# Selective scan on one core: decays from differences of running sums in two-part fp32r products

## The chip, the cores and the metric

The program runs on one core of a Trainium2 chip. Its engines work side by side, each through its own queue in order: TensorE (PE, matrix products into PSUM), VectorE (DVE), ScalarE (ACT, activation functions from tables), GpSimd (POOL) and SyncE (SP, which here only starts transfers). The metric is the device time of one execution in microseconds (us), as the median of several runs; lower is better. PE's weight loads are shown apart from its products, as PEld. An fp32 product shows as two passes with a weight load each, an fp32r product as one.

## The reference

Two layers over 4 x 2048 tokens of width 256: attention with LoRA and a small mixture of experts, then a chunked selective state-space scan and a second mixture of experts. Only the scan is touched by the change. Its core, cut to what matters (one head group, 4 heads of width 128, state width 64, `dA = dt * A`, all negative):

```
cum = jnp.cumsum(dA, axis=2)
seg = cum[:, :, :, None, :] - cum[:, :, None, :, :]
decay = jnp.where(tri[None, None, :, :, None], jnp.exp(seg), 0.0)
scores = jnp.einsum('bcin,bcjn->bcij', Cc, Bc)
att = scores[..., None] * decay * dtc[:, :, None, :, :]
y_intra = jnp.einsum('bcijh,bcjhp->bcihp', att, xc)
```

The kernel scans in sub-tiles of 128 tokens, so for each sub-tile and head it needs a 128 x 128 table `exp(cum_i - cum_j)`, masked to the triangle.

## The kernel before

The program is a row of stages; `scan_phase` is the fifth, and runs from about 3590 to 4468 us of the span. It goes through 16 chunks of 512 tokens (4 batches of 4 chunks, the batch being the hardware loop, the chunks written out in it). I call the work of one pass a turn. In turn `i` the kernel scans chunk `i`, in 4 sub-tiles s = 0 to 3; it projects, convolves and gates chunk `i + 1`; and it normalizes chunk `i + 2`. Each engine's order within a turn is written out by hand.

PE writes most results into four PSUM banks `sc_ps_a`, used in rotation. The list `A_TURN` says in which order: its names are `xT` (inputs transposed), `dt` (step sizes), `seg` (decay exponents), `ct` (convolution inputs), `z` (gates), `gT` (gated rows transposed), `out` (output projection), `cum` (sums), `uT` (normalized inputs transposed). PE may write entry k once ACT has read entry k - 4 (`into`, semaphore `a_out`), and ACT reads entry k once PE has written it (`take`, `a_done`). So PE and ACT follow the same list and are never more than four entries apart.

The decays of a sub-tile are made like this. POOL computes the step sizes by a series of short operations (`softplus_argument`, `softplus_series`), and its last operation gives `dA` (L1520). ACT multiplies a strictly lower triangular mask by `dA`, head by head (`segment_mask`, L1773, four activations a sub-tile). PE multiplies each of the four masks by an upper triangular one in fp32 (`decays`, L1966), which gives the exponents. ACT takes their exponential (L1784, `sc_decay`), DVE multiplies by the scores (L1658, `sc_att`), and PE uses the result in `own` (L2002).

The names that matter below: `own` 0 is PE's product for sub-tile 0 of the turn; DVE adds it up (L1675), whereupon POOL gates the row (`gate`, L1534). POOL's order in a turn is gate 0, `second_root` (L1488), in the first turn of a batch the weights `wob` (L1527), the step sizes, `dA`, gates 1, 2 and 3. PE needs gate s for `gT`s (L2018). In PE's order `gT1` comes just before `sums` (L1958) and, before the change, `seg0` of the next chunk. Near the turn's end PE does z3 (L1943), gT2, uT0, the scores of the next chunk (L1976), uT1 (L1927), the state of sub-tile 3 (L2011), gT3, out2, out3 (L2027) and xT0 (L1984). The product for out3 waits until ACT has copied gT3 (L1829). The step-size products (L1950, four columns each) and `seg1` come right after the next turn's start.

ACT's exponential and its Silu lie in different function tables; a change from one to the other shows as ACT_TABLE_LOAD. Copy, Identity and Square need no change.

## Time and profile before

| what | value |
|---|---|
| median of 3 runs | 5099.54 us (5083.22 to 5102.6) |
| the profiled execution | 5088.73 us |
| its span, first to last instruction | 5087.2 us |
| mean granted clock of TensorE | 0.942 of 2.4 GHz |
| scan stage, about | 3590 to 4468 us of the span |
| PE busy over the whole span | 92% |
| DVE, ACT, POOL busy over the whole span | 84%, 69%, 27% |

Times within the trace are counted from the span's start. A busy share says how much of a stretch an engine worked; a wait says who came last. In the scan a turn takes 48.5 to 55.8 us, by ACT's copies of the step sizes at 3711.6, 3761.8, 3812.1, 3860.8 and 3916.5 us and so on.

### The profile page before, as it was taken

What the parts mean: (1) busy time and instruction counts of PE and PEld (TensorE: products, weight loads), DVE (VectorE), ACT (ScalarE), POOL (GpSimd) and SP (SyncE); (2) the same over time, 40 slices, a digit from 0 to 9 for tenths busy, and PEclk for the clock granted to TensorE, in tenths of its full rate; (3) what the DMA queues carried; (4) which work ended last, traced back from release to release, by engine and by line L of the source; (5) the groups of instructions that cost most, each with busy time, mean ns of one, the idle gap of its engine ahead of it and who ended that gap; (6) DMA issues with size and microseconds to landing.
All of it is one profiled execution on the core that took longest, in us unless ns stands there. A gap on an engine that the chain in (4) does not pass through costs nothing. (4 is left out here: it accounts for less than half of the span.)

```text
span 5087.2 us, 109400 instructions
## 1 busy us (share of the span) xinstructions
PE 4686.5 (92%) x35413; PEld 2578.5 (51%) x35413; DVE 4257.3 (84%) x6858; ACT 3489.3 (69%) x6724; POOL 1383.5 (27%) x1285
## 2 busy tenths in 40 slices
PE   5869999999999999999999879999699999956998
PEld 4723333333333333333333367777466666655887
DVE  5769999999999999999999868887677877875554
ACT  2438888888888888888888722322477777844554
POOL 1121111111111111111111133333334344445776
PEclk8959999999999999999999989999799999956999
DMA  4962222122222222222222111111000000044452
GB/s 157 345 146 43 52 44 49 39 47 52 44 47 42 46 52 43 44 44 45 55 44 44 33 51 41 37 50 37 22 25 24 28 20 23 25 162 148 164 164 94
DMA packets 236446, 340.01 MB, mean 67 GB/s; under 512 B 60199, under 2 KB 169762, under 8 KB 227340
## 3 DMA queue, kind: packets, MB, share of 16 engines
q1 hardware_dynamic: 219760, 275.26, 22.3%
q0 software_dynamic: 16192, 58.43, 3.1%
q8 instruction: 277, 4.54, 0.4%
q14 instruction: 217, 1.78, 0.1%
HBM read 205.49 MB, written 136.18 MB: 67 GB/s over the span
## 5 line engine op out<-in xcount | busy, mean ns | idle before, releaser
L816 DVE TENSOR_REDUCE at_mxp<-at_ps_m 128x2 f32<-128x1024 f32 x2092 | 2524.5, 1221 | 72.9 <-PE at_ps_m L869 53.0
L747 ACT ACTIVATE at_prob<-at_ps_s 128x512 f32<-128x512 f32 x4100 | 2228.2, 596 | 326.8 <-PE at_ps_s L859 261.7
L879 PE MATMUL at_ps_o<-at_prob,at_vs 128*32 128x256 f32 x16384 | 1313.9, 392 | 14.1 <-ACT at_osum L753 14.1
L859 PE MATMUL at_ps_s<-at_qs,at_ks 51*128 51x512 f32 x4100 | 1036.5, 500 | 5.2 <-ACT at_prob L747 5.2
L869 PE MATMUL at_ps_m<-at_ks,at_qs 49*128 49x512 f32 x4184 | 856.3, 405 | 46.5 <-DMA at_ks<-t_alibi 35.7
L859 PEld LDWEIGHTS at_ps_s<-at_qs,at_ks 51*128 51x128 f32 x4100 | 384.9, 183 | 856.6 <-ACT at_prob L747 856.1
L879 PEld LDWEIGHTS at_ps_o<-at_prob,at_vs 128*32 128x32 f32 x16384 | 323.1, 108 | 775.3 <-issue 388.5
L574 POOL TENSOR_TENSOR at_total<-at_total,at_minus 128x16 f32<-128x16 f32 x65 | 190.4, 2929 | 1118.1 <-DMA at_total<-at_osum 1118.1
L869 PEld LDWEIGHTS at_ps_m<-at_ks,at_qs 49*128 49x128 f32 x4184 | 404.0, 190 | 67.9 <-DMA at_ks<-t_alibi 36.1
L68 DVE TENSOR_TENSOR ex_hidc<-ex_hid,ex_hidc 128x512 fp32r<-128x512 f32 x128 | 158.0, 1245 | 168.9 <-ACT ex_hid L2561 168.9
L1321 PE MATMUL mi_ps_f<-mi_w,mi_act 128*128 128x256 f32 x1024 | 252.6, 391 | 15.7 <-DVE mi_acc L1179 15.7
L1244 ACT ACTIVATE mi_act<-mi_ps_h,mi_b 128x512 f32<-128x512 f32 x130 | 89.5, 688 | 233.2 <-PE mi_ps_h L1310 232.8
L1179 DVE SCALAR_TENSOR_TENSOR mi_acc<-mi_ps_f,mi_mask,mi_acc 128x256 f32<-128x256 f32 x512 | 215.1, 475 | 36.6 <-PE mi_ps_f L1321 32.9
L1310 PE MATMUL mi_ps_h<-mi_hTc,mi_w1c 128*128 128x512 f32 x780 | 236.5, 441 | 7.6 <-POOL mi_hTc L68 7.6
L569 POOL TENSOR_TENSOR at_nparts<-at_nmax,at_nparts 128x16 fp32r<-128x16 f32 x65 | 14.4, 222 | 798.5 <-DVE at_nparts L823 798.5
L2560 ACT ACTIVATE ex_hidc<-ex_ps_h,ex_b 128x512 fp32r<-128x512 f32 x128 | 88.2, 689 | 202.9 <-PE ex_ps_h L2591 202.9
L1321 PEld LDWEIGHTS mi_ps_f<-mi_w,mi_act 128*128 128x128 f32 x1024 | 196.5, 196 | 58.9 <-DVE mi_acc L1179 29.4
L1634 DVE SCALAR_TENSOR_TENSOR sc_cv<-sc_xc,sc_conv_w,sc_cv 128x512 f32<-128x512 f32 x255 | 198.6, 812 | 19.0 <-issue 5.9
L578 POOL TENSOR_TENSOR at_onorm<-at_osum,at_weight 128x512 f32<-128x512 f32 x65 | 83.4, 1283 | 338.0 <-DMA at_weight<-t_inverse 338.0
L1310 PEld LDWEIGHTS mi_ps_h<-mi_hTc,mi_w1c 128*128 128x128 f32 x780 | 152.1, 199 | 44.8 <-issue 14.0
L1937 PE MATMUL sc_ps_a<-sc_uT,sc_win 128*128 128x512 f32 x340 | 166.7, 624 | 0.9 <-ACT sc_uT L1821 0.9
L1534 POOL TENSOR_TENSOR sc_g<-sc_ysum,sc_sz 128x512 f32<-128x512 f32 x64 | 83.0, 1297 | 293.1 <-DVE sc_ysum L1675 293.1
(317 smaller groups left out, 6443.5 us busy)
## 6 DMA issues: line engine op xcount, KB each, us to landing
t_parts<-pr_parts SPq DMA_DIRECT2D x64, 512.0 KB, 7.1
at_ks<-t_parts SPq DMA_DIRECT2D x102, 256.0 KB
t_buf<-at_blank POOLq DMA_DIRECT2D x64, 384.5 KB, 3.2
at_qs<-t_parts SPq DMA_DIRECT2D x96, 256.0 KB
at_vs<-t_v SPq DMA_DIRECT2D x17, 1024.0 KB, 5.0
ex_rest<-t_buf SPq DMA_DIRECT2D x16, 1026.0 KB, 5.3
t_v<-pr_vaug SPq DMA_DIRECT2D x64, 256.0 KB, 5.5
first_w<-in_fw SPq DMA_DIRECT2D x16, 1024.0 KB, 7.6
```

Source lines behind the costliest of these rows:

```text
L68: return eng.tensor_tensor(out, src, upper.bitcast(F32), ALU.subtract)
L574: nc.gpsimd.tensor_tensor(total[:, :], total[:, :], minus[:, :], ALU.pow).then_inc(inverted, 1)
L747: nc.scalar.activation(prob[0 if up is None else (t + 1) % 2][:, j, :], ps_s[bank][:, :], ACT.Exp).then_inc(s_read, 1)
L816: nc.vector.tensor_reduce(out[:, s4, k + i, 2 * pair:2 * pair + 2], ps_m[i][:, :, :], AX.X, ALU.max).then_inc(mx_read, 1)
L859: nc.tensor.matmul(ps_s[bank][:, :], ks[s][a:a + QROWS, j // 2, t1 * P:(t1 + 1) * P], qs[s][a:a + QROWS, j // 2, c * T:(c + 1) * T], start ...
L869: last = nc.tensor.matmul(ps_m[i][:, a, :], qs[s][a * 64:a * 64 + MXR, pair, q0:q0 + P], ks[s][a * 64:a * 64 + MXR, pair, (k + i) * T:(k + ...
L879: last = nc.tensor.matmul(ps_o[32 * j:32 * j + 32, q0:q1], vs[s][:, t, 32 * j:32 * j + 32], prob[t % 2][:, j, q0:q1], start=(t == 0 and ha ...
L1179: last = nc.vector.scalar_tensor_tensor(acc[:, s, :], ps_f[pair][:, j, :], mask[h][:, s, e:e + 1], acc[:, s, :], ALU.mult, ALU.add)
L1310: last = nc.tensor.matmul(ps_h[e % 2][:, :], w1c[a][:, e, k, :], hTc[h][r][:, k, :], start=(k == 0 and n == 0), stop=(k == KD - 1 and n == 2))
L1321: last = nc.tensor.matmul(ps_f[pair][:, j, :], act_e[e][:, s * P:(s + 1) * P], w2[:, e, :], start=True, stop=True)
L1634: last = nc.vector.scalar_tensor_tensor(cv[:, ct, :], xc[h][:, ct, k:k + T], conv_w[:, ct, k:k + 1], cv[:, ct, :], ALU.mult, ALU.add)
L1937: last = nc.tensor.matmul(bank[:, :], win[:, k, DI + ct * P:DI + (ct + 1) * P], uT[h][:, k, :], start=(k == 0), stop=(k == KD - 1))
```

## The change

The decay exponents come from differences of running sums. With `run` the running sum of `dA` over the tokens (rows: 4 sub-tiles x 4 heads), an exponent is `run[i] - run[j]`. To keep precision in fp32r, `run` is split in two parts, a rounded one and the rest, as 48 rows (part, sub-tile, head; the middle part is zero).

- POOL writes `dA` twice (into parts 0 and 2 of `dA_rows`).
- PE's `sums` gets a fourth fp32 product, 48 x 128, which gives the running sums as rows.
- ACT's `sums` copies these rows twice (once rounded to fp32r), and after its exponential drains and scales the rounded ones by -1 in part 2 only.
- POOL's new `running_rows`, between gate 2 and gate 3, adds the two into `run` (48 x 128) and spreads them over heads into `spread_run` (48 x 512).
- PE's `decays` is two accumulating fp32r products with 512 columns and 48 rows, in place of four fp32 products with 128 columns.
- ACT's `segment_mask`, four times four activations a turn, is gone.
- Without the mask, exponents above the diagonal are positive; DVE caps the decay at 1 in the instruction that applies the scores, whose triangle is masked as before.
- `seg0` of the next chunk moves behind z3 in PE's order, in ACT's order and in the rotation of banks.
- Ahead of the loop SP loads four small tables, and POOL converts two of them.

```diff
-          + ["gT1", "cum", "seg0", "z2", "out1", "z3", "gT2", "uT0", "uT1", "gT3", "out2", "out3", "xT0"])
+          + ["gT1", "cum", "z2", "out1", "z3", "seg0", "gT2", "uT0", "uT1", "gT3", "out2", "out3", "xT0"])
...
+                sp.dma_start(decay[0][0:CR, :, :], x["own_rows"].rearrange("r (s c) -> r s c", s=SUB)).then_inc(rows_in, 16)
...
-                    nc.gpsimd.tensor_tensor(dA[h][:, :, :], dts[h][:, :, :], a_neg[:, :].unsqueeze(1).to_broadcast([P, SUB, NH]), ALU.mult).then_inc(dA_done, 1)
+                    for part in (0, 2):
+                        last = nc.gpsimd.tensor_tensor(dA_rows[h][:, part, :, :], dts[h][:, :, :], a_neg[:, :].unsqueeze(1).to_broadcast([P, SUB, NH]), ALU.mult)
+                    last.then_inc(dA_done, 1)
+
+                def running_rows(n, h):
+                    pool.wait_ge(run_out, n + 1)
+                    nc.gpsimd.tensor_tensor(run[h][:, :], run_m[:, :], run_f[:, :], ALU.add)
+                    pool.drain()
+                    nc.gpsimd.tensor_tensor(spread_run[h][:, :, :], run[h][:, :].bitcast(F32).unsqueeze(1).to_broadcast([CR, NH, P]),
+                                            head_rows[:, :].unsqueeze(2).to_broadcast([CR, NH, P]), ALU.mult).then_inc(run_set, 1)
...
                         gate(i, h, 2, True)
+                        running_rows(i + 1, 1 - h)
                         gate(i, h, 3, True)
...
-                    nc.vector.tensor_tensor(att[r][:, :, :], decay[r][:, :, :], sm[r][:, :].unsqueeze(1).to_broadcast([P, NH, P]), ALU.mult).then_inc(att_done, 1)
+                    nc.vector.scalar_tensor_tensor(att[r][:, :, :], decay[r][:, :, :], 1.0, sm[r][:, :].unsqueeze(1).to_broadcast([P, NH, P]), ALU.min, ALU.mult).then_inc(att_done, 1)
...
-                def segment_mask(n, h, s, used):
...
                 def sums(turn, h):
                     bank = take(turn, "cum")
+                    nc.scalar.copy(run_r[:, :], bank[0:CR, P:2 * P])
+                    nc.scalar.copy(run_f[:, :], bank[0:CR, P:2 * P])
                     nc.scalar.activation(ex[h][:, :, :, :], bank[:, 0:3 * SUB * NH].rearrange("p (a s h) -> p a s h", a=3, s=SUB), ACT.Exp).then_inc(a_out, 1)
+                    act.drain()
+                    nc.scalar.activation(run_m[:, :], run_r[:, :].bitcast(F32), ACT.Copy, scale=minus_low[:, 0:1]).then_inc(run_out, 1)
...
                         gate_squares(i, h, 1)
-                        decays(turn, i + 1, 0, True)
-                        segment_mask(i + 1, 1 - h, 1, place(turn, "seg3")[0])
                         gates(turn, 1 - h, 2)
...
                         gates(turn, 1 - h, 3)
+                        decays(turn, i + 1, 0, True)
                         gated_columns(turn, 2)
...
-                    pe.wait_ge(seg_set, i * SUB + s + 1)
-                    for k in range(NH):
-                        last = nc.tensor.matmul(bank[:, k * P:(k + 1) * P], segm[s % 2][:, k, :], upper[:, :], start=True, stop=True)
-                    last.then_inc(a_done, 1)
+                    pe.wait_ge(run_set, i + 1)
+                    nc.tensor.matmul(bank[:, :], own_rows[:, s, :], spread_run[h][:, :, :].rearrange("r h c -> r (h c)"), start=True, stop=False)
+                    nc.tensor.matmul(heads(bank), run[h][:, :], minus_rows[:, s, :].unsqueeze(2).to_broadcast([CR, NH, P]), start=False, stop=True).then_inc(a_done, 1)
```

On ACT, from the gate z3 (L1808) to the copy of gT3 (L1829), the order before was this. `sc_sz` is a Silu, `sc_xs` the Silu of the convolution.

```order
L1808 ACTIVATE sc_sz<-sc_ps_a 128x512
L1829 COPY sc_gT<-sc_ps_a 128x512
L1821 ACTIVATE sc_uT<-sc_ps_a,sc_nb,sc_nw 128x512
L1813 ACTIVATE sc_xs<-sc_cv 128x512
L1821 ACTIVATE sc_uT<-sc_ps_a,sc_nb,sc_nw 128x512
L1829 COPY sc_gT<-sc_ps_a 128x512
```

The same stretch, from z3 to the copy of gT3, in the changed kernel:

```order
L1831 ACTIVATE sc_sz<-sc_ps_a 128x512
L1807 ACT_TABLE_LOAD
L1807 ACTIVATE sc_decay<-sc_ps_a 128x512
L1852 COPY sc_gT<-sc_ps_a 128x512
L1844 ACTIVATE sc_uT<-sc_ps_a,sc_nb,sc_nw 128x512
L1836 ACT_TABLE_LOAD
L1836 ACTIVATE sc_xs<-sc_cv 128x512
L1844 ACTIVATE sc_uT<-sc_ps_a,sc_nb,sc_nw 128x512
L1852 COPY sc_gT<-sc_ps_a 128x512
```

The exponential of `seg0` now stands between two Silus, with a table load on each side of it. Before, it shared a table with the exponentials of `seg3` and `sums`.

On PE, from gT1 to z2, the order before was:

```order
L2018 MATMUL sc_ps_a<-ident,sc_g 128x128 x4
...
L1958 MATMUL sc_ps_a<-sc_dA,upper 128x16
L1958 MATMUL sc_ps_a<-sc_dA,sc_lower 128x16
L1958 MATMUL sc_ps_a<-sc_dA,ones 128x16
...
L1966 MATMUL sc_ps_a<-upper,sc_segm 128x128 x4
...
L1943 MATMUL sc_ps_a<-sc_win,sc_uT 128x512 x2
```

and in the changed kernel:

```order
L2033 MATMUL sc_ps_a<-ident,sc_g 128x128 x4
...
L1974 MATMUL sc_ps_a<-sc_dA,upper 128x16
L1974 MATMUL sc_ps_a<-sc_dA,sc_lower 128x16
L1974 MATMUL sc_ps_a<-sc_dA,ones 128x16
L1975 MATMUL sc_ps_a<-upper,sc_dA 48x128
...
L1959 MATMUL sc_ps_a<-sc_win,sc_uT 128x512 x2
```

A fourth product of `sums` has come in, and `seg0` has left this place for the one behind z3.

## Rows read from the trace of the kernel before

**Rows 1.** Stretches of the scan: busy time by engine, clock, DMA share, GB/s.

```profile
3700.00:3800.00 100.00, 99.50 (x490) 66.83 (x491) 79.01 (x206) 78.10 (x192) 42.03 (x60) 0.97 0.08 25
```

**Rows 2.** Waits of PE, then of ACT, from 3700 to 4400 us.

```profile
PE sc_ps_a L2018 <- POOL sc_g L1534: 8.9, 8, 2.4
...
ACT sc_segm L1773 <- POOL sc_dA L1520: 25.5, 14, 3.6
```

**Rows 3.** Timeline of PE, one turn: start, us, engine, line, tiles, count [wait].

```profile
3767.63 1.05 PE L2002 MATMUL sc_ps_y<-sc_xdt,sc_att 128*128 128x128 f32 x8
...
3788.77 1.09 PE L2011 MATMUL sc_ps_st<-sc_xdt,sc_btw 128*64 128x128 f32 x8
3790.11 0.63 PE L2018 MATMUL sc_ps_a<-ident,sc_g 128*128 128x128 f32 x4 [0.25 <-POOL sc_g L1534]
...
3791.17 1.14 PE L1966 MATMUL sc_ps_a<-upper,sc_segm 128*128 128x128 f32 x8
3792.14 1.88 PE L1943 MATMUL sc_ps_a<-sc_win,sc_uT 128*128 128x512 f32 x4
...
3797.73 1.88 PE L1943 MATMUL sc_ps_a<-sc_win,sc_uT 128*128 128x512 f32 x4
...
3802.98 3.62 PE L2027 MATMUL sc_ps_a<-sc_wob,sc_gT 128*128 128x256 f32 x16
3806.44 0.60 PE L1984 MATMUL sc_ps_a<-ident,sc_xs 128*128 128x128 f32 x4
...
3816.32 1.05 PE L2002 MATMUL sc_ps_y<-sc_xdt,sc_att 128*128 128x128 f32 x8
```

**Rows 4.** Timeline of POOL in the same turn, gate 0 to gate 2.

```profile
3769.49 1.27 POOL L1534 TENSOR_TENSOR sc_g<-sc_ysum,sc_sz 128x512 f32<-128x512 f32 x1 [10.79 <-DVE sc_ysum L1675]
...
3772.66 0.22 POOL L1497 TENSOR_TENSOR sc_zp<-sc_ez,sc_two 128x16 f32<-128x16 f32 x1
...
3788.52 0.22 POOL L1520 TENSOR_TENSOR sc_dA<-sc_dts,sc_a_neg 128x16 f32<-128x16 f32 x1
3788.69 1.27 POOL L1534 TENSOR_TENSOR sc_g<-sc_ysum,sc_sz 128x512 f32<-128x512 f32 x1
3792.65 1.37 POOL L1534 TENSOR_TENSOR sc_g<-sc_ysum,sc_sz 128x512 f32<-128x512 f32 x1 [2.69 <-DVE sc_ysum L1675]
```

**Rows 5.** Timeline of PE in the expert stage: six fp32r products with 512 columns.

```profile
4699.92 1.54 PE L2591 MATMUL ex_ps_h<-ex_bTc,ex_w1c 128*128 128x512 f32 x6
4701.30 1.60 PE L2603 MATMUL ex_ps_y<-ex_w2c,ex_hidc 128*128 128x256 f32 x12
```

**Rows 6.** Timeline of ACT in the same turn, z2's table load and z3 to gT3.

```profile
3794.12 1.28 ACT L1808 ACT_TABLE_LOAD   x1
3795.41 0.60 ACT L1808 ACTIVATE sc_sz<-sc_ps_a 128x512 f32<-128x512 f32 x1
...
3799.65 0.60 ACT L1808 ACTIVATE sc_sz<-sc_ps_a 128x512 f32<-128x512 f32 x1 [1.20 <-PE sc_ps_a L1943]
3800.14 0.58 ACT L1829 COPY sc_gT<-sc_ps_a 128x512 f32<-128x512 f32 x1
3800.61 0.80 ACT L1821 ACTIVATE sc_uT<-sc_ps_a,sc_nb,sc_nw 128x512 f32<-128x512 f32 x1
3801.28 0.63 ACT L1813 ACTIVATE sc_xs<-sc_cv 128x512 f32<-128x512 f32 x1
3801.80 0.79 ACT L1821 ACTIVATE sc_uT<-sc_ps_a,sc_nb,sc_nw 128x512 f32<-128x512 f32 x1
3803.18 0.59 ACT L1829 COPY sc_gT<-sc_ps_a 128x512 f32<-128x512 f32 x1 [0.59 <-PE sc_ps_a L2018]
```

**Rows 7.** First turn of a batch: PE's timeline at gT1, then stretches with their clock.

```profile
3891.24 1.05 PE L2018 MATMUL sc_ps_a<-ident,sc_g 128*128 128x128 f32 x4 [2.40 <-POOL sc_g L1534]
...
3895.07 3.40 PE L1943 MATMUL sc_ps_a<-sc_win,sc_uT 128*128 128x512 f32 x4
...
3891.00:3898.00 7.00, 6.76 (x22) 5.21 (x23) 3.57 (x6) 4.44 (x12) 1.46 (x2) 0.52 0.00 1
3761.60:3765.00 3.40, 3.40 (x10) 2.14 (x10) 3.23 (x12) 3.37 (x9) 0.00 (x0) 0.50 0.50 146
```

More of the change, by code:

```diff
@@ L1906, in batch @@
                         projected(turn, h, 3)
-                        segment_mask(i + 1, 1 - h, 2, place(turn, "seg0")[0])
                         skip_inputs(turn, i + 1, 1 - h, 0, True)
@@ L2078, in _ @@
                         sums(turn, n, g1)
-                        decays(turn, n, 0)
                         gates(turn, g1, 2)
@@ L2084, in _ @@
                         gates(turn, g1, 3)
+                        decays(turn, n, g1, 0)
                         gated_columns(turn, 2)
```

54 lines of the change are left out of this document (33 added, 21 removed).

## The prediction

> **What bounds the kernel now.** I read the stretches of the scan first. In a typical hundred microseconds PE is busy for 99.5, DVE 79.0, ACT 78.1 and POOL 42.0 [rows 1]. That looks like a stage bound by PE alone, in which each microsecond taken from PE is a microsecond won. So I went to the waits. PE waits for one thing, POOL's gated row before gT1: 8.9 us in total, 8 times, at most 2.4 [rows 2]. That is little, but it says that at one place POOL arrives as late as PE does. The reader is to see this in the two timelines of one turn.
>
> In PE's timeline `own` 0 starts at 3767.63. The state of sub-tile 2 starts at 3788.77 and takes some 1.1, and gT1 starts at 3790.11 with a wait of 0.25 ahead of it [rows 3]. In POOL's timeline gate 0 starts at 3769.49, the step sizes at 3772.66, `dA` at 3788.52 and gate 1 at 3788.69, which takes 1.27 and ends at 3789.96 [rows 4]. PE's gT1 starts 0.15 later. From `own` 0 to gT1, stretch A, there are thus two paths of nearly the same length. One is PE's own work, 22.2 us. The other goes `own` 0, DVE, gate 0, the step sizes, `dA`, gate 1, gT1, and takes 22.5 us; almost nothing of it is PE's. The rest of the turn, stretch B, from gT1 at 3790.11 to the next `own` 0 at 3816.32, is 26.2 us [rows 3], and in it PE runs without waits. In the first turn of a batch POOL also makes `wob`, and PE's wait is 2.40 [rows 7].
>
> **The change, part by part.** *PE, the decays.* Eight fp32 passes of one sub-tile occupy PE from 3791.17 to 3792.14, 0.97 us [rows 3]. The new form is two fp32r products with 512 columns. The nearest row has six of them from 4699.92 to 4701.30, so 0.23 each and 0.46 for two [rows 5]. It contracts over 128 rows and not 48, and it repeats no column; I take it as it stands. Each sub-tile gives back 0.51. The bounds are 0.40 for the pair, if few rows were cheaper, and 1.7 if it ran at the rate of the fp32 form (four passes with 512 columns take from 3792.14 some 1.7 [rows 3]). The fourth product of `sums` is two more fp32 passes with 128 columns: 2 x 0.97 / 8 = 0.24.
>
> *Stretch A* holds the decays of sub-tiles 2 and 3, so PE's path falls from 22.2 to 21.2. POOL's path does not fall. It gets a second `dA` operation: the first starts at 3788.52 and the next operation at 3788.69, so one costs 0.17 [rows 4]; I take 0.2. It ends stretch A at 22.7. So A becomes 0.2 longer, and PE's wait at gT1 grows from 0.25 to about 1.5. The 1.0 us given back by PE is lost there.
>
> *Stretch B, PE's side.* It holds the decays 0 and 1 and `sums`: -0.51 - 0.51 + 0.24 = -0.8.
>
> *Stretch B, ACT's side.* Here the two table loads matter. A load takes 1.28 and begins only when the activation ahead has ended: from 3794.12 to the Silu at 3795.41 [rows 6]. I lay out the new order with the spacings of the rows. Since `seg0` has left and the fourth sum has come, z3 ends 0.97 - 0.24 = 0.73 earlier, and ACT's Silu of z3 starts at 3799.65 - 0.72 = 3798.93. It takes 0.60, the load 1.29, the exponential 0.49 to the next start (the spacing from z3 to gT2), gT2 0.47, uT0 0.80 (its full length, since a load follows), the load 1.29, the Silu 0.52, uT1 about 0.67 and gT3's copy 0.59 [rows 6]. The sum is 6.72, so gT3 is copied at 3805.65. PE's out3 needs it. PE would come to out3 at half of the way from 3802.98 to 3806.44, which is 3804.71, less 0.73 and plus 0.46 for `seg0` in its new place: 3804.44 [rows 3]. So PE waits for ACT by 1.2 us, where before it did not wait: ACT had gT3 copied at 3803.77 [rows 6] and out3 came 0.9 later. Out3 starts 0.94 later than before. The decays of sub-tile 1 then give back 0.51, and stretch B becomes 0.4 longer in place of 0.8 shorter.
>
> The Trainium skill, in "ScalarE: Activation LUTs", "What ACT_TABLE_LOAD costs", puts a switch at some 1283 ns of load and some 1380 ns of drain. The load agrees with the row's 1.28. Of the drain the row shows nothing beyond the end of the activation ahead, and the row decides. By the page two switches would cost 2.8 us more than I have put down, in each turn.
>
> *What is hidden.* The masks that go, sixteen activations a turn, free ACT, but ACT waited for `dA` at one of them anyway (25.5 us in 14 turns [rows 2]), and no wait of PE for a mask stands among PE's waits. ACT already stood idle for 1.20 before z3's Silu [rows 6]; that, and the two masks that went from the stretch ahead of it, covers the three new small activations in `sums`. `running_rows` costs POOL about as much as a gate, 1.27 [rows 4], and a fraction for the addition. Gate 2 ends at 3794.02 [rows 4], some 4 us after gT1, and `seg0` is asked for after z3, 8.6 us after gT1: it has 3 us to spare, and gate 3 is asked for later. DVE's cap stands in an instruction of the same size; DVE is busy for 79.0 of 100 [rows 1]. If the cover were gone, each tenth of a microsecond on DVE would count four times a turn, 6 us in all. The first chunk has the new chain sums, ACT, POOL, PE in the open in place of two masks: +1 us.
>
> **Sum.** A turn becomes 0.2 + 0.4 = 0.6 us longer, 16 turns 10, with the first chunk 11 us.
>
> *The clock.* In the stretch after the wait of 2.40 the granted clock was 0.52, the half level of 1.2 GHz, for about 7 us, and four passes took 3.40 in place of 1.88 [rows 7]. In another stretch after the small step-size products it was 0.50 for 3.4 us [rows 7]. A wait of 1.5 followed by the small products of `sums` is a case between. I cannot tell from rows whether it brings the clock down: nothing if it never does, and about 1.6 a turn if it does once in each (3.4 us at half speed), 26 us. I take two turns in five, 10 us.
>
> So +21 us. The profiled execution took 5088.7 and the median is 5099.5, with 5083.2 as the lowest; the four values centre at 5094, and I add to that: **5115 us**.
>
> **The rivals.**
>
> 1. *PE alone is the bound, and all it gives back is won.* For it: PE is busy for 99.5 of 100. Against it: the 0.25 us wait, which leaves no room in stretch A. It would need POOL's path to shorten. Four times 0.51 less 0.24 is 1.8 a turn, -29 us in all: 5065.
> 2. *ACT comes in time at gT3.* If a table load could run while PE's z3 is awaited, one of the two would be hidden, B would be shorter by 0.8 and A longer by 0.2: -10 us, 5084. Against it: the load stands behind the Silu of z3, and needs its end.
> 3. *The new waits bring the clock down in nearly every turn.* PE now waits 1.5 at gT1 and 1.2 before out3. With 1.6 to 3.2 us a turn lost at half speed, on top of 11: +37 to +62, 5131 to 5156. It decides from about one turn in two on. For it: the row after 2.40 us. Against it: most waits now are shorter than that one.
> 4. *The decays don't get cheaper.* A pair at 1.7 us adds 0.7 per sub-tile to a turn's B in place of giving 0.51 back: about 2.4 a turn, over 40 us slower. Against it: fp32r at 0.23 in the expert stage [rows 5].
>
> **How the numbers follow.** The forecast (10 us from the two waits, 0 to 26 from the clock, so 5105 to 5131) has 0.60. A third of that, 0.18, lies above +0.5%. Rival 1 has 0.09, rival 2 0.08, rival 3 0.20 and rival 4 0.03. Half a per cent is 25 us, about what a measurement of this kernel can tell from no change. Faster by more: rival 1, 0.09. Slower by more: 0.18 + 0.20 + 0.03 = 0.41. Within: 0.42 + 0.08 = 0.50. The range leaves out rival 1 and the upper end of rivals 3 and 4: 5080 to 5150.
>
> **What would show it.** In the changed profile I expect: gT1 starting 22.7 after `own` 0, with a wait for POOL of about 1.5 in each turn; six table loads a turn where there were four; out3 starting right after ACT's copy of gT3, and some 1.7 us behind its place; decays of about 0.46 on PE; PE's busy share in the scan down to about 95 of 100; and a turn of 49 to 51 us without the batch's first. I am wrong if gT1 keeps its place relative to PE's own work, if POOL's path is shorter than 22 us, or if the copy of gT3 comes before PE is through out2. I am also wrong in size if the half clock appears after gT1 in all turns or in none.

## The result, and the profile after

The changed kernel takes 5141.54 us (median of 5 runs, 5136.32 to 5158.21), against 5099.54 us before (median of 5 runs). That is 42 us longer by the medians. The ratio is 1.0102, with a 95% interval of 1.0081 to 1.0123; it is estimated from all runs and isn't the quotient of the two medians, which is 1.0082. The forecast was 5115 with a range of 5080 to 5150, some 21 us more than the 5094 that it was added to. So the sign was right and the size was half of what came, and a part of the loss lies in a stage that the forecast had no term for.

First the span and the mean granted clock of the profiled execution after.

```profile
core 0: 5140.0 us, clock 0.938
```

Then the busy row of a hundred microseconds of its scan: PE, PEld, DVE, ACT and POOL busy, PE's clock, the DMA share and GB/s.

```profile
3740.00:3840.00 100.00, 96.71 (x434) 60.51 (x434) 80.17 (x199) 73.72 (x165) 43.04 (x64) 0.97 0.08 25
```

PE was busy for 99.50 [rows 1] and is now busy for 96.71: it has less work and waits more. The waits of PE in the scan, 3700 to 4400 us (total, times, longest), say for whom:

```profile
PE sc_ps_a L2033 <- POOL sc_g L1554: 24.5, 14, 5.8
PE sc_ps_a L2042 <- ACT sc_gT L1852: 11.0, 13, 0.9
```

The first row is the wait at gT1, 8.9 us before [rows 2]. The second, ahead of out3, is new. Here is one turn in PE's timeline: `own` 0, the pair of sub-tile 2, gT1, `sums`, z2, `seg0`, gT2, the last two projections, the step sizes with the pair of sub-tile 1, and the next `own` 0.

```profile
3784.68 1.05 PE L2017 MATMUL sc_ps_y<-sc_xdt,sc_att 128*128 128x128 f32 x8
3785.66 0.49 PE L1981 MATMUL sc_ps_a<-sc_spread_run,sc_own_rows 48*128 48x512 f32 x1
3786.00 0.38 PE L1982 MATMUL sc_ps_a<-sc_minus_rows,sc_run 48*128 48x512 f32 x1
3786.30 1.98 PE L1953 MATMUL sc_ps_a<-sc_uT,sc_win 128*128 128x512 f32 x4
...
3807.26 0.63 PE L2033 MATMUL sc_ps_a<-ident,sc_g 128*128 128x128 f32 x4 [0.86 <-POOL sc_g L1554]
3807.73 0.29 PE L1974 MATMUL sc_ps_a<-sc_dA,upper 128*128 128x16 f32 x2
...
3808.75 1.98 PE L1959 MATMUL sc_ps_a<-sc_win,sc_uT 128*128 128x512 f32 x4
...
3816.25 0.49 PE L1981 MATMUL sc_ps_a<-sc_spread_run,sc_own_rows 48*128 48x512 f32 x1
3816.58 0.37 PE L1982 MATMUL sc_ps_a<-sc_minus_rows,sc_run 48*128 48x512 f32 x1
3816.89 0.66 PE L2033 MATMUL sc_ps_a<-ident,sc_g 128*128 128x128 f32 x4
...
3820.48 1.89 PE L2042 MATMUL sc_ps_a<-sc_wob,sc_gT 128*128 128x256 f32 x8
3823.16 1.99 PE L2042 MATMUL sc_ps_a<-sc_wob,sc_gT 128*128 128x256 f32 x8 [0.78 <-ACT sc_gT L1852]
3824.99 0.60 PE L1999 MATMUL sc_ps_a<-ident,sc_xs 128*128 128x128 f32 x4
...
3827.07 1.85 PE L1966 MATMUL sc_ps_a<-sc_win,sc_uT 128*128 128x4 f32 x16
3828.84 0.49 PE L1981 MATMUL sc_ps_a<-sc_spread_run,sc_own_rows 48*128 48x512 f32 x1
...
3829.76 1.45 PE L2026 MATMUL sc_ps_st<-sc_xdt,sc_btw 128*64 128x128 f32 x8
3831.14 4.98 PE L1953 MATMUL sc_ps_a<-sc_uT,sc_win 128*128 128x512 f32 x8
3835.96 1.05 PE L2017 MATMUL sc_ps_y<-sc_xdt,sc_att 128*128 128x128 f32 x8
```

Stretch A, from 3784.68 to 3807.26, is 22.58; the forecast was 22.7. The pair of sub-tile 2 takes PE from 3785.66 to 3786.30, 0.64 and not 0.46. From gT1's follower `sums` (3807.73) to z2 (3808.75) are 1.02. Stretch B, from 3807.26 to 3835.96, is 28.70. It holds a slow piece: eight passes with 512 columns take 4.98 from 3831.14, where the four at 3786.30 take 1.98. In the window around the turn's start PE is busy throughout, and its granted clock (the third number from the end) is 0.66 on average, so for a part of it at the lower of its two levels, 1.2 GHz and not 2.4:

```profile
3828.80:3833.80 5.00, 5.00 (x17) 2.97 (x18) 3.85 (x16) 3.02 (x8) 0.00 (x0) 0.66 0.50 164
```

And ACT in the same turn, from z3 to the copy of gT3:

```profile
3816.36 0.60 ACT L1831 ACTIVATE sc_sz<-sc_ps_a 128x512 f32<-128x512 f32 x1 [1.53 <-PE sc_ps_a L1959]
3816.97 1.28 ACT L1807 ACT_TABLE_LOAD   x1
3818.26 0.60 ACT L1807 ACTIVATE sc_decay<-sc_ps_a 128x512 f32<-128x512 f32 x1
3818.76 0.58 ACT L1852 COPY sc_gT<-sc_ps_a 128x512 f32<-128x512 f32 x1
3819.22 0.80 ACT L1844 ACTIVATE sc_uT<-sc_ps_a,sc_nb,sc_nw 128x512 f32<-128x512 f32 x1
3820.04 1.28 ACT L1836 ACT_TABLE_LOAD   x1
3821.33 0.63 ACT L1836 ACTIVATE sc_xs<-sc_cv 128x512 f32<-128x512 f32 x1
3821.87 0.76 ACT L1844 ACTIVATE sc_uT<-sc_ps_a,sc_nb,sc_nw 128x512 f32<-128x512 f32 x1
3822.53 0.57 ACT L1852 COPY sc_gT<-sc_ps_a 128x512 f32<-128x512 f32 x1
```

This is the chain of [rows 6] with two table loads in it. It ends at 3823.10, and out3 starts 0.06 later.

I add up the two profiled executions, whose spans are 52.8 apart. Up to the scan's first product they differ by 9.8; the diff touches nothing of what PE does there, and over all profiles of this study its length goes from 3601 to 3621, in no order that follows the edits. Without it the two are 43.0 apart. The scan, from PE's first to its last product, takes 894.8 in place of 861.5: +33.4. In it the time up to the first `own` 0 is 5.5 longer, fifteen stretches A are 3.8 longer (351.1 against 347.3), fifteen stretches B are 22.9 longer (441.3 against 418.4), and the rest is 1.2. The route stage, which the change doesn't touch either, takes 163.7 in place of 152.2: +11.5. What lies behind it gives 1.9 back.

### The profile page after: what moved, and what is told of

It reads as the page before. It is cut to its first block and busy times, and to the rows that moved or that the text cites. A ratio compares the mean times of both kernels' runs of the same rounds, so it can differ in the third digit from the quotient of the medians.

```text
span 5140.0 us, 108585 instructions
## 1 busy us (share of the span) xinstructions
PE 4696.3 (91%) x35057; PEld 2546.1 (50%) x35057; DVE 4270.2 (83%) x6858; ACT 3466.2 (67%) x6539; POOL 1412.5 (27%) x1340
## 5 line engine op out<-in xcount | busy, mean ns | idle before, releaser
L1953 PE MATMUL sc_ps_a<-sc_uT,sc_win 128*128 128x512 f32 x340 | 183.6, 677 | 0.9 <-ACT sc_uT L1844 0.9
```

The source lines that it names most:

```text
L1953: last = nc.tensor.matmul(bank[:, :], win[:, k, DI + ct * P:DI + (ct + 1) * P], uT[h][:, k, :], start=(k == 0), stop=(k == KD - 1))
```

## The experiments

The table has what I read from each. A and B are sums over fifteen turns. "Quiet B" is the shortest B of a turn, without a stretch at the half clock; for the changed kernel and for e11, where every turn has one, it is 28.69 less the 1.64 that such a stretch costs in the kernel before (27.84 against 26.20) and in e3 (28.73 against 27.08). "Half" is the time in the fifteen turns at which the clock's records stand at the half level, and "falls" in how many of the fifteen turns the clock fell behind the step-size products or beside them, at the turn's start (some expectations count the sixteenth, unfinished turn as well: 14 and 4 for 13 and 3). Times are in us. They were taken in five groups, in each of which the kernel before ran as well: it took 5099.5 beside after, 5091.1 beside e1 to e4, 5084.5 beside e5 to e8, 5092.7 beside e11 to e14 and 5092.2 beside e15 to e17. So between groups the ratios are to be compared and not the times.

| kernel | time | ratio to before, 95% | A | B | quiet B | half | falls | route |
|---|---|---|---|---|---|---|---|
| before | 5099.5 | 1 | 347.3 | 418.4 | 26.20 | 51.2 | 9 | 152.2 |
| after | 5141.5 | 1.0102 (1.0081 to 1.0123) | 351.1 | 441.3 | 27.05 | 75.1 | 13 | 163.7 |
| e1_no_loads | 5126.7 | 1.0061 (1.0038 to 1.0083) | 350.5 | 418.0 | 26.00 | 61.4 | 8 | 163.7 |
| e2_move_alone | 5136.4 | 1.0083 (1.0063 to 1.0104) | 347.0 | 459.8 | 27.17 | 92.2 | 11 | 153.6 |
| e3_short_series | 5076.2 | 0.9972 (0.9957 to 0.9986) | 327.7 | 423.6 | 27.08 | 34.1 | 10 | 151.6 |
| e4_few_steps | 5089.6 | 0.9997 (0.9985 to 1.0008) | 350.5 | 397.9 | 25.72 | 27.3 | 0 | 163.8 |
| e5_before_few_steps | 5070.8 | 0.9952 (0.9930 to 0.9975) | 349.7 | 381.8 | 24.86 | 20.5 | 0 | 153.3 |
| e6_split_steps | 5124.8 | 1.0076 (1.0054 to 1.0098) | 350.3 | 425.1 | 26.94 | 44.4 | 3 | 163.9 |
| e7_seg0_beside_seg1 | 5127.5 | 1.0064 (1.0040 to 1.0088) | 350.6 | 440.4 | 25.95 | 119.5 | 14 | 163.2 |
| e8_all | 5081.8 | 0.9985 (0.9964 to 1.0005) | 325.0 | 430.9 | 26.37 | 81.9 | 13 | 164.4 |
| e11_after_filler | 5130.6 | 1.0065 (1.0041 to 1.0090) | 350.6 | 441.6 | 27.05 | 75.1 | 13 | 151.8 |
| e12_before_filler | 5086.0 | 0.9983 (0.9969 to 0.9997) | 347.8 | 411.4 | 26.20 | 37.5 | 5 | 151.7 |
| e13_after_pool | 5084.7 | 0.9986 (0.9965 to 1.0008) | 324.8 | 434.3 | 27.31 | 44.4 | 7 | 151.8 |
| e14_before_pool | 5079.0 | 0.9980 (0.9967 to 0.9993) | 332.3 | 416.2 | 26.35 | 34.1 | 6 | 153.6 |
| e15_seg0_last | 5096.9 | 1.0001 (0.9982 to 1.0019) | 325.1 | 448.8 | 26.45 | 102.4 | 13 | 151.8 |
| e16_seg0_last_split | 5077.5 | 0.9963 (0.9944 to 0.9982) | 325.0 | 425.3 | 26.30 | 54.6 | 8 | 151.7 |
| e17_after_pool_unsplit | 5087.4 | 0.9995 (0.9974 to 1.0015) | 324.8 | 434.2 | 27.47 | 41.0 | 11 | 151.7 |

The theory is the prediction's: A is bound by POOL, B by ACT's loads, and the rest is the clock. The rivals are its rivals.

### The loads, and the move

**e1_no_loads.** In the loop, `seg0`'s exponential becomes a copy.

```diff
-                    nc.scalar.activation(decay[s % 2][:, :, :], heads(bank), ACT.Exp).then_inc(a_out, 1)
+                    nc.scalar.activation(decay[s % 2][:, :, :], heads(bank), ACT.Copy if s == 0 and turn is not None else ACT.Exp).then_inc(a_out, 1)
```

> The changed kernel, but in the loop ACT copies the exponents of seg0 in place of taking their exponential (the decays of sub-tile 0 are left out of the result), so the two table loads around it go: four a turn again. If the late copy of gT3 costs PE the time before out3, that wait goes and stretch B falls by about 1.2 us a turn at equal clock, 18 us in all: about 5122. If ACT's loads are beside the point and the loss is the clock's or the new products', stretch B stays and so does the time, about 5141. The wait for POOL at gT1 stays at 0.9 either way.

The quiet B fell from 27.05 to 26.00, and PE's only wait left in the scan was POOL's:

```profile
PE sc_ps_a L2033 <- POOL sc_g L1554: 23.9, 14, 5.8
```

So the two loads cost 1.05 a turn, some 16 us in all. The sum of B fell by more, 23.3, since the clock fell in 8 turns and no longer in 13; the ratios are 0.41% apart, some 21 us. Rival 2, ACT in time, falls. The quiet B of 26.00 says one thing more: without the loads, the cheaper decays make B only 0.2 shorter than before (26.20), where the prediction had 0.8.

**e2_move_alone.** The kernel before, with only `seg0` moved behind z3 on PE and ACT.

```diff
-          + ["gT1", "cum", "seg0", "z2", "out1", "z3", "gT2", "uT0", "uT1", "gT3", "out2", "out3", "xT0"])
+          + ["gT1", "cum", "z2", "out1", "z3", "seg0", "gT2", "uT0", "uT1", "gT3", "out2", "out3", "xT0"])
```

> The kernel before, with nothing but seg0 moved behind z3 on PE, on ACT and in the banks; masks and fp32 products stay. If the loads are the cause, they come with the move: PE waits about 0.7 us before out3, 11 us in all, and a half-clock stretch more here and there: 5110 to 5120. If the two-part form is the cause, this kernel is as fast as the one before: 5100.

The waits of PE, 3700 to 4440 us, beside the old one for POOL at gT1:

```profile
PE sc_ps_a L2027 <- ACT sc_gT L1829: 12.9, 14, 1.0
PE sc_ps_in L1991 <- issue: 6.2, 3, 2.5
```

And ACT's load for `seg0` in one turn, with what it waited for:

```profile
4296.92 1.28 ACT L1784 ACT_TABLE_LOAD   x1 [0.36 <-PE sc_ps_a L1966]
```

The quiet B rose from 26.20 to 27.17. The move alone, without any cheaper decay, makes the whole of B's quiet loss. Its ratio is four fifths of the changed kernel's (1.0083 of 1.0102), though its route stage is the short one; but that holds more than the quiet loss, since B's sum, 459.8, is the largest of all, with 92.2 us at the half clock, and the time came out above its forecast of 5110 to 5120. The `issue` row is one that the changed kernel doesn't have: PE stood for some 2 us where its loop goes back, three times, and the turns there were 57 long. The load row says more: the load started only when the product was through whose result its activation reads. Between 3700 and 4400 us ACT waited so ahead of a load nine times, 3.2 us in all.

### POOL's path

**e3_short_series.** The changed kernel with three terms fewer in the step-size series.

```diff
-                    nc.gpsimd.tensor_scalar(zp[:, :, :], zw[:, :, :], 1.0 / 17, None, ALU.mult)
-                    for k in range(15, 1, -2):
+                    nc.gpsimd.tensor_scalar(zp[:, :, :], zw[:, :, :], 1.0 / 11, None, ALU.mult)
+                    for k in range(9, 1, -2):
```

> The changed kernel with three of the eight steps of POOL's series left out (the step sizes lose their last terms): POOL's path is some 3.5 us shorter. If POOL ends stretch A, it falls from 22.5 to 21.6 in the plain turns, where PE's own work ends it, and by some 3.5 in the first turn of a batch, where the half-clock stretch after gT1 should go too: 34 us in all, about 5107. If POOL is not what PE waits for, nothing moves: 5141.

A fell to 21.66 in all but the first turns of a batch, and to 22.2 to 22.4 there. Then PE's wait for POOL was all but gone, and out3's stayed:

```profile
PE sc_ps_a L2042 <- ACT sc_gT L1852: 12.0, 14, 0.9
PE sc_ps_a L2033 <- POOL sc_g L1554: 2.1, 3, 0.7
```

So POOL does bound A. It costs 0.8 to 1.1 in a plain turn and some 3 in a batch's first, where the half clock behind gT1 went with it. The time fell below the forecast of 5107, to 5076.2, since more than A moved: B's sum fell by 17.7, with the clock falling in 10 turns, and the route stage was the short one, 151.6 in place of 163.7.

### The step-size products and the clock

**e4_few_steps** and **e5_before_few_steps.** The sixteen passes of four columns become four passes of sixteen, in the changed kernel and in the one before.

```diff
-                    for s in range(SUB):
-                        for k in range(KD):
-                            last = nc.tensor.matmul(bank[:, s * NH:(s + 1) * NH], uT[h][:, k, s * P:(s + 1) * P], win[:, k, RT * P:ZX], start=(k == 0), stop=(k == KD - 1))
+                    for k in range(KD):
+                        last = nc.tensor.matmul(bank[:, 0:SUB * NH], uT[h][:, k, 0:P], win[:, k, ZX - SUB * NH:ZX], start=(k == 0), stop=(k == KD - 1))
```

> The changed kernel with the step-size products cut from sixteen small passes to four (other step sizes come out). PE has 1.3 us less to do in stretch B: 21 us in all, about 5120, if the clock falls as before. If the half-clock stretch after them is brought on by these small passes, it goes as well, 1.6 us in fourteen turns: 44 us in all, about 5097.

> The kernel before with the step-size products cut from sixteen small passes to four, as was done to the changed kernel, which then took 5089.6 (other step sizes come out). If a part of the loss is that the clock falls after these passes in more turns of the changed kernel (14 of 15 against 9 of 15 in the profiles), this kernel gains less from the edit: 1.3 us in each turn and 1.6 in nine, 36 us in all, about 5055, and the distance between the two kernels shrinks from about 45 to about 30. If the clock has no part in the loss, the distance stays at 45: about 5045.

In neither kernel did any turn show the half clock behind the step sizes. The quiet B fell by 1.3, which is the time of the passes, and the sums of B by 43 and 37. So e4 shows the second of its two forecasts (5097; it took 5089.6). What stays between the two is B's 0.9 a turn, and the route stage. The distance of the ratios is 0.45%, some 23 us, in place of 1.02%; 11 us of it are the route stage. That the distance shrinks is as forecast. The time of e5 was not: the scan is 35 us shorter, as the forecast of 5055 asks, but in the profile the part ahead of the scan is 18 us longer than in the kernel before, and the median came at 5070.8.

**e6_split_steps.** The products of the changed kernel in two halves, with the carried product and xT1 between them.

```diff
+                        steps(turn, g1, (0, 1))
                         carried(i, h, 0)
                         token_inputs(turn, i, h, 1)
-                        steps(turn, g1)
+                        steps(turn, g1, (2, 3))
```

> The changed kernel with the step-size products in two halves, one ahead of the product with the carried state and one in the old place. PE's work is the same. If the clock falls because all sixteen small passes come together, it falls there less often: 1.6 us in up to thirteen turns, 20 us in all, about 5120. If what lowers the clock is something else near the turn's start, nothing moves: 5141.

The clock fell at this place in 3 turns of 15, where it had fallen in 13; B's sum went from 441.3 to 425.1. Of these 16 us the ratios show 0.26%, some 13 us (their intervals overlap), and the time of 5124.8 is near the forecast of 5120. The clock is worth that much here, and the order of a few short products moved it. The three falls that stay are twice as long as most before, 6.8 us at the half level, and cost 3.3 each. The runs below show that the same split need not win anything (e13 beside e17).

### Other places for seg0

**e7_seg0_beside_seg1.** `seg0` goes just ahead of `seg1`, into the next turn, so that one load serves both.

```diff
-A_TURN = (["xT1", "dt", "seg1", "ct4",
-          + ["gT1", "cum", "z2", "out1", "z3", "seg0", "gT2",
+A_TURN = (["xT1", "dt", "seg0", "seg1", "ct4",
+          + ["gT1", "cum", "z2", "out1", "z3", "gT2",
```

> The changed kernel with seg0 moved on, to just ahead of seg1 in the next turn, on PE, ACT, DVE and in the banks; everything is computed. Its exponential then shares a table with that of seg1: four loads a turn. If the loads cost 1.1 us a turn in stretch B, as with the copied exponents, this kernel has B at 26.0 without a half-clock stretch and takes about 5125. If taking the exponential itself matters, or the later decays of sub-tile 0 hold up own 0, B stays at 27.1 or grows: 5141 or more.

The quiet B fell to 25.95 and out3 did not wait. But only one turn was free of the half clock at its start; in most B was 28.9. What the loads gave came back as clock: B's sum is 440.4 in place of 441.3. The median of 5127.5 is near the 5125 that the theory asked for, but it didn't come by the theory's way. In the profile the scan is 9 us shorter than the changed kernel's, and 6 of these lie ahead of the first `own` 0.

**e8_all.** The same, with the split, and two edits to POOL's order: `wob` is made ahead of gate 0, and gate 1 is done inside the series.

```diff
+                        if c == 0:
+                            weigh_rows(b, i)
                         gate(i, h, 0, old)
                         second_root(i + 2)
-                        if c == 0:
-                            weigh_rows(b, i)
                         softplus_argument(i + 1)
-                        softplus_series(i + 1, 1 - h)
-                        gate(i, h, 1, old)
+                        softplus_series(i + 1, 1 - h, lambda: gate(i, h, 1, old))
```

> Four edits on the changed kernel: seg0 beside seg1, the step-size products in two halves, the weights wob made before gate 0 instead of after it, and gate 1 put into the series of the step sizes. If the account by stretches holds, A is PE's own 21.7, also in the first turn of a batch, B is 26.0 and few turns have a half-clock stretch: 47.7 a turn against 51.2, and 55 in the first turns: 75 us less in all, about 5065, faster than the kernel before. If the stretches were bound by something else, the gain is under 40 us.

A was 21.66 in every turn, the batch's first too. So another order of the same work on POOL is enough to free A; less work, as in e3, is not needed. The half clock stayed at the turn's start, in 13 of 15 turns and most often for 6.8 us. So the forecast of 5065 was missed by 17 us.

### The route stage

Here are POOL's rows in the route stage's second chunk, before and then after. Up to this place the two run alike.

```profile
4511.15 1.04 POOL L2171 TENSOR_TENSOR ro_rstd<-ro_ve,ro_mhalf 128x4 f32<-128x4 f32 x1 [2.36 <-DVE ro_ve L2217]
4512.19 0.19 POOL L2176 TENSOR_TENSOR ro_target<-ro_slot,ro_away 128x4 uint32<-128x4 uint32 x1
4513.60 1.21 POOL L2179 DMA_INDIRECT t_buf<-ro_row,ro_target  x1 [1.22 <-issue]
```

```profile
4554.15 1.04 POOL L2186 TENSOR_TENSOR ro_rstd<-ro_ve,ro_mhalf 128x4 f32<-128x4 f32 x1 [2.36 <-DVE ro_ve L2232]
4558.03 0.43 POOL L2191 TENSOR_TENSOR ro_target<-ro_slot,ro_away 128x4 uint32<-128x4 uint32 x1 [2.83 <-issue]
4559.70 1.04 POOL L2194 DMA_INDIRECT t_buf<-ro_row,ro_target  x1 [1.23 <-issue]
```

After, POOL stands for 2.83 us behind its first operation and waits for nothing that the profile shows. In the view of the DMA queues of this stretch, 4552 to 4560, there is a row that the same stretch of the kernel before doesn't have (packets, MB, share):

```profile
q14 instruction: 1, 0.01, 0.2%
```

A piece of POOL's instructions is loaded there, 8192 bytes, 40 us into the stage. From then on the stage runs in another rhythm: POOL issues a chunk's transfers every 10.4 us, where it was every 9.4. In the waits of 4570 to 4660, DVE stands for the transfers of the chunk four before, whose buffer it needs:

```profile
DVE ro_row L2242 <- DMA t_buf<-ro_row,ro_target: 11.3, 9, 2.9
```

**e11_after_filler** and **e12_before_filler.** Tiny memsets ahead of the stage on POOL: 24 in the changed kernel, 34 in the one before.

```diff
+                for k in range(24):
+                    nc.gpsimd.memset(spare[:, k:k + 1], -0.5)
                 nc.gpsimd.memset(mhalf[:, :], -0.5)
```

> The changed kernel with 24 tiny memsets of a spare tile ahead of the first operation of POOL in the route stage, where POOL waits for 5.3 us anyway. Nothing else is touched. Theory (where the code lies): the route stage took 163.7 us in the changed kernel and 152.2 in the one before, although its text is the same in both. In the trace of the changed kernel a piece of POOL's instructions (8192 bytes) is loaded in the second chunk of the stage's loop, POOL stands still for 2.83 us there, and from then on each chunk takes 10.4 us in place of 9.4. In the kernel before no piece is loaded there. The filler moves the loop by 24 instructions, past the border of the piece: I expect a route stage of about 152 to 154, no stall of 2.8, and about 11 us less in all, some 5130 (ratio 1.008). Rival (the stage is longer because of what the scan leaves behind, data in DRAM or the clock): the route stage stays at 164 and the time at 5141.

> The kernel before with 34 tiny memsets at the same place, which is about the number of instructions that the change adds to POOL ahead of the route stage. Theory (where the code lies): the border of a piece now falls into the loop as in the changed kernel, and the route stage takes about 164 us in place of 152: about 5110, ratio 1.002. Rival: it stays at 152 and the ratio at 1.000. Should my count of the instructions be off by ten or more, the border may miss the loop and nothing changes; a trace shows where the piece was loaded.

With the filler the stage of the changed kernel took 151.8, and POOL's row at the same place lost its stall:

```profile
4556.39 0.19 POOL L2192 TENSOR_TENSOR ro_target<-ro_slot,ro_away 128x4 uint32<-128x4 uint32 x1
4557.80 1.21 POOL L2195 DMA_INDIRECT t_buf<-ro_row,ro_target  x1 [1.22 <-issue]
```

The ratio fell from 1.0102 to 1.0065, more than the 12 us of the stage, though their intervals overlap, and A and B were the same to half a microsecond (350.6 and 441.6). So the 11.5 us come from where the code lies and not from what the scan does. The other runs agree: the six kernels with a load 40 us into the stage (after, e1, e4, e6, e7, e8) take 163.2 to 164.4 for it, and all others 151.6 to 153.6. e12 missed: the stage stayed at 151.7, although in its trace too a piece of POOL's code was loaded 41 us into the stage. A load in the loop is thus not enough; presumably it matters at which instruction POOL runs dry, which no run tests. I have not shown why the later rhythm holds once it has begun. e12 also measures something else. Its scan has the same order as before, and yet B summed to 411.4 and the half clock to 37.5, so these two vary by some 7 and 14 us from one execution to the next. And its ratio of 0.9983 (0.9969 to 0.9997) lies below 1, with scan and route stage as before: a difference of 0.2% between two kernels is not to be explained by their edits.

The Trainium skill, in "Runtime: NRT & Kernel Launch", "Instruction fetch mechanics", calls the cost of crossing from one piece of code to the next mostly hidden. The stall here is such a crossing, in the second chunk of the loop's first pass and ahead of its first jump back. The measurement differs from the page: it was 2.83 us at once and 11.5 in the end.

### With POOL out of the way

**e13_after_pool.** The changed kernel in its own order, with both edits to POOL's order, the split and the filler.

> The changed kernel with its order kept on PE and ACT, and four edits: wob made ahead of gate 0, gate 1 put into the step-size series, the step-size products in two halves, and the filler of 24. Theory: stretch A falls to 21.7 in every turn, the first of a batch too (as in the run in which the series was shorter, A summed to 328 in 15 turns in place of 351), B stays at 27.1 with a half-clock stretch after the products in a third of the turns (425 in place of 441), the route stage at 152. Together 23 + 16 + 11 = 50 us less than the changed kernel: about 5092, ratio about 1.000. Rival (the half clock comes back elsewhere, as it did with seg0 beside seg1): B at 440 and more, 5105 or above.

**e14_before_pool.** The kernel before with both edits to POOL's order.

> The kernel before with two of the edits: wob ahead of gate 0, gate 1 inside the step-size series. Theory: POOL's path no longer ends stretch A. A falls from 22.5 to PE's own 22.2 in most turns, and in the first turn of a batch the wait of 2.4 and the half-clock stretch behind it (3.3) go: 4 x 5.5 + 11 x 0.3 = 25 us less, about 5070, ratio 0.995. Rival (PE's own work bounds A, and the wait is only what is left over): the first turns win the wait but keep the half clock, about 10 us less, ratio 0.998. If A in the changed kernel with the same edits is 21.7 and here 22.2 and more, the 0.5 between them is what the cheaper decays of sub-tiles 2 and 3 are worth once POOL is out of the way.

**e17_after_pool_unsplit.** As e13 without the split, and so the partner of e14.

> The changed kernel with wob ahead of gate 0, gate 1 inside the series and the filler, and nothing else: the pair to the kernel before with the same two POOL edits (quiet turn 22.16 + 26.55 = 48.7). What is left between the two is the change itself with POOL out of the way: A 0.5 less (two pairs), B 0.9 more, with some 0.4 x 16 = 6 us, and the half clock. Theory: A 21.66, B 27.4 quiet, a half-clock stretch behind the step sizes in 12 to 15 turns, ratio 1.002 to 1.005. Rival (POOL's path was the only reason why the changed kernel lost): ratio 0.997 or below.

In e14 A is 22.15 to 22.16 in each turn, in e17 21.65 to 21.66: the two pairs in A save 0.49, so 0.245 each where the prediction had 0.51. In B e17 is 1.0 longer in a typical quiet turn (27.5 against 26.5). Both lost the wait in a batch's first turn, and from the second batch on the half clock behind it, as the windows around and behind gT1 of such a turn show, first the changed kernel and then e17 (the clock is the third number from the end):

```profile
3912.60:3919.60 7.00, 7.00 (x19) 4.49 (x20) 1.92 (x4) 3.89 (x9) 2.61 (x3) 0.54 0.01 2
```

```profile
3892.00:3899.00 7.00, 6.93 (x38) 4.75 (x37) 6.74 (x17) 4.16 (x11) 3.61 (x9) 1.00 0.00 1
```

The rival of e17, that POOL's path was the only reason for the loss, asked for 0.997 or below. With POOL gone from both, the change is 0.15% behind (0.9995 against 0.9980), within their intervals, and does not gain; its route stage, with the filler, is even the shorter one by 2 us. But the forecast for e17, 1.002 to 1.005, was too high as well. e13 was forecast at 5092 and came at 5084.7. e14 was forecast at 5070 and came at 5079: 15 us of A were won, but B's sum hardly fell (418.4 to 416.2), since its quiet turn grew from 26.20 to 26.5 and two of the falls were of twice the length. Its 0.9980 is hardly less than what e12 shows without any edit to the scan (0.9983), so what the two edits to POOL's order are worth in the kernel before stands in the trace and not in the times.

e13 has the split and e17 doesn't, and B's sum is the same, 434.3 and 434.2. In e13 the clock fell in 7 turns and not in 11, but four of these falls were twice as long. So here the split won nothing.

**e15_seg0_last** and **e16_seg0_last_split.** `seg0` goes behind gT3 on PE and behind the last Silu on ACT, so that the next turn's `seg1` finds its table. Both have the POOL edits and the filler, e16 the split too.

```diff
-          + ["gT1", "cum", "z2", "out1", "z3", "seg0", "gT2", "uT0", "uT1", "gT3", "out2", "out3", "xT0"])
+          + ["gT1", "cum", "z2", "out1", "z3", "gT2", "uT0", "uT1", "gT3", "seg0", "out2", "out3", "xT0"])
```

> The changed kernel with wob ahead of gate 0, gate 1 inside the step-size series, the filler of 24 in the route stage, and seg0 moved on: on PE behind gT3, ahead of out2; on ACT behind the last Silu of the convolution, so that seg1 of the next turn finds its table loaded (4 loads a turn in place of 6); DVE applies it in the next turn. The step-size products stay together. Theory (the two loads between z3 and gT3 are what takes B's gain): A 21.66 as in the run with these POOL edits, out3 no longer waits, and B in a quiet turn is 27.4 less 0.9 to 1.1, 26.4: a quiet turn of 48.1, against 48.7 in the kernel before with the same POOL edits. With about the same number of half-clock stretches, 0.6 x 16 = 10 us less than that kernel, 5065 to 5075, ratio 0.995 to 0.997. Rival (the half clock follows, as with seg0 beside seg1): B at 28 and more in most turns, ratio 1.000 or above.

> The same with the step-size products in two halves around the carried product and xT1. Theory: the halves cost a tenth of a microsecond and halve the number of half-clock stretches behind them, as in the changed kernel (14 to 4 of 15): another 5 to 10 us, 5060 to 5070. Rival: as in the run with all POOL edits and the split, about every second turn still has one, some of them twice as long, and the two kernels are the same within 0.2%.

In e16 PE goes through the turn's end without a wait. These are its rows from `seg0` to the first half of the step sizes:

```profile
3747.56 0.49 PE L1982 MATMUL sc_ps_a<-sc_spread_run,sc_own_rows 48*128 48x512 f32 x1
3747.90 0.38 PE L1983 MATMUL sc_ps_a<-sc_minus_rows,sc_run 48*128 48x512 f32 x1
3748.20 3.72 PE L2043 MATMUL sc_ps_a<-sc_wob,sc_gT 128*128 128x256 f32 x16
3751.76 0.60 PE L2000 MATMUL sc_ps_a<-ident,sc_xs 128*128 128x128 f32 x4
3752.20 0.95 PE L1966 MATMUL sc_ps_a<-sc_win,sc_uT 128*128 128x4 f32 x8
```

The quiet turn is 48.1 in e15 and 47.95 in e16, with e8's 48.0 the shortest of all kernels with the full step sizes; `seg0`'s place in the changed kernel costs 1.0 a turn (e17's quiet turn is 49.1). The theory was right there. What e15 makes of it is the rival: 13 of 15 turns show the half clock at the turn's start, which costs 3.2 in each, and the kernel is no faster than the one before. e16 with its split has 8 such turns, seven of them in a row at the end, and is 0.37% faster than the kernel before, the only one with the change and the full step sizes whose interval lies below 1 (0.9944 to 0.9982). It still missed its forecast of 5060 to 5070, with 5077.5. The split was forecast at 5 to 10 us and is worth 19 here, in the same group of runs, where it was worth 13 in e6 and nothing in e13. With POOL out of the way PE has one small wait left in both, for `dA` ahead of `sums`, 2 to 3 us in all. Windows around the turn's start in e15 and in a turn of e16 without it:

```profile
3815.00:3821.00 6.00, 6.00 (x22) 4.21 (x22) 4.18 (x15) 2.20 (x8) 0.00 (x0) 0.56 0.51 175
```

```profile
3755.50:3760.50 5.00, 5.00 (x21) 3.02 (x21) 3.93 (x13) 3.09 (x10) 0.00 (x0) 1.00 0.53 173
```

PE is busy throughout in both, and the DMA share is the same. Its clock is at the lower level for most of the one window, and at the upper throughout the other.

## Why the prediction was right in kind and wrong in size

The forecast was half of what came, and two of its steps failed. The sum had no term for anything outside the scan, without a reason given, and the route stage took 11.5 us more. And stretch B was put 0.4 longer a turn and is 0.85 longer, since the pair, the fourth product of `sums` and PE's wait ahead of out3 all cost more than was put down. One by one:

- **Stretch A, +0.2 and bound by POOL: right.** In a plain turn it is 22.45 to 22.80 in place of 22.30 to 22.68, 0.1 more on average, and in a batch's first turn 0.6 to 0.7 more. e3, e8 and e14 show that POOL ends it. The wait at gT1 is 0.72 to 1.08 in plain turns and not 1.5, since PE's own work fell by 0.49 and not by 1.0.
- **The pair at 0.46: wrong, the first mis-sized term.** It took 0.64 between products of 512 columns in fp32, 0.55 at sub-tile 1, and the net gain in A was 0.245 a sub-tile. The row that I took it from is a run of six equal fp32r products with 128 rows [rows 5]; here each pair stands alone between fp32 products. The bounds, 0.40 to 1.7, held it.
- **The fourth product of `sums` at 0.24: wrong, the second.** `sums` went from 0.60 to 1.02 between neighbours, so 0.42. I had taken the eighth part of the decays' time per pass.
- **ACT's chain of 6.72 to the end of gT3's copy: right.** It is 6.74 in the timeline. The two loads take what B had gained, and e1 and e2 show it from both sides. But PE's wait ahead of out3 costs more than its 0.78 on the row: from out2's start to xT0's it is 4.51, against 3.46 before, so 1.05, which is also what e1 gave back. Together with the two terms above B came out 0.85 longer (26.20 to 27.05), not 0.4: 7 us of the miss over sixteen turns.
- **The clock, +10: right in sum by luck, at another place.** I had put it behind the longer wait at gT1. There it did not appear in any plain turn, which the prediction had named as a sign of a wrong size. It appeared behind the step-size products, in 13 of 15 turns in place of 9, at 1.64 each and sometimes more. Of B's 22.9, 12.8 are the quiet turn and some 10 this. e4, e5, e6 and e16 show that it hangs on the short products and their order. Why it came more often after this change stays open. PE's new wait ahead of out3, which comes some 4 us before the step sizes, is a candidate: among the kernels with `seg0` in one of its two places of before and after and without the split, those that have this wait show 10 to 13 falls (after, e2, e3, e11, e17), and those without it 5 to 9 (before, e1, e12, e14). Against it stands e15, which has the same order of short products at the turn's start and no such wait, and shows 13. And two executions of one order differ by 4 (before and e12), so that single counts prove little.
- **The first chunk, +1: wrong.** It took 61.6 up to the first `own` 0 in place of 56.1. But the kernels with masks had 55.2 to 58.7, and those with pairs and `seg0` in the first chunk 57.1 to 61.6. The two ranges overlap, so that how much of the 5.5 is the change isn't shown.
- **Nothing outside the scan: wrong, the largest miss.** The sum had no line for the stages that the diff doesn't touch. The change adds instructions to POOL ahead of the route stage, which moves that stage's loop against the borders at which code is loaded: 11.5 us, which e11 took away. Why the stage's later rhythm holds is open.
- **The rivals.** Rival 1 (PE alone, 5065) needed a shorter path on POOL; e17 gave it that and came to 5087, since B's loss stays. Rival 2 fell with e1. Rival 3 had the size (5131 to 5156) and in part the cause: the half clock came in nearly every turn, but at the step sizes, and it is only 10 of the 42 us. Rival 4 is out: the pair is cheaper than what it replaced.

So of the 26 us by which the forecast missed (5141.5 against 5115), 11.5 are the route stage, 7 the two prices on PE and the true cost of the wait in B, and 4 the first chunk, by the two profiles; 2 were given back behind the route stage. The rest, 5.5, is the base: I had added to 5094, and the median of before is 5099.5.

## What to carry to other kernels

Where two engines arrive at a place together, work taken from one of them is worth nothing there: first shorten the other's path, here by moving one gate and one weighting in POOL's order, with the same work. An activation that needs another table belongs where its neighbours already use that table; moved between two of another kind it cost two loads of 1.28 us ahead of a product that PE waits for, a microsecond a turn. And a stage that the diff doesn't touch can still change: compare stage by stage before explaining a difference by the edit.

## What the runs showed of the hardware that I had not expected

- PE's clock fell to 1.2 GHz though PE did not stand still (busy 5.00 of 5.00 us at a mean clock of 0.66, after). It did so behind sixteen passes of four columns and the short products that follow them, in 13 turns of 15; in other kernels with the same sixteen passes in one piece, in 5 to 14. With four passes of sixteen columns it did not fall there in any turn of two kernels (e4, e5). With the sixteen split into two halves it fell in 3 turns and not in 13 (e6), but elsewhere in 7 and not in 11 (e13, e17), with nothing won. A fall costs 1.64 us, at times 3.3.
- A table load did not run ahead of the data. In e2 it began only when PE's product for its activation was through, after 0.36 of waiting, and so in nine places.
- A wait of 0.78 on a row of PE cost 1.05 from neighbour to neighbour (out2 to xT0, 4.51 against 3.46).
- 24 tiny memsets made one stage 12 us shorter (163.7 to 151.8, after and e11): a piece of POOL's code was no longer loaded in the middle of its loop. With such a load 41 us into the stage in place of 40, another kernel lost nothing (e12).
- The same scan, in the same order, differs by 7 us and by 14 us of half-clock time between two executions (before and e12); and even by the medians of 10 and 24 runs they are 0.13% apart.
